# Writing the softmax maxima into the query rows of a strip instead of into a joint buffer

## The reference, cut to what matters

```python
scores = jnp.einsum('bqhd,khd->bhqk', Q, K) * SCALE
attn = jax.nn.softmax(scores, axis=-1)
out = jnp.einsum('bhqk,khd->bqhd', attn, V).reshape(B, QL, HIDDEN)
```

## Time and profile before

| what | value |
|---|---|
| median of 3 runs | 1769.31 us (1768.32 to 1775.3) |
| the profiled execution's own time | 1772.17 us |
| its span | 1770.3 us |
| granted clock of PE, mean | 0.987 |
| PE busy in the span | 96% |
| DVE busy | 79% |
| ACT busy | 65% |
| POOL busy | 30% |

### The profile page before, as it was taken

The page is one execution under the profiler, slowest core; times in us unless marked ns, Lnnn a source line. Parts: engine busy times, 40 slices in busy tenths (PEclk is TensorE's granted clock), DMA queues, the critical chain, the costliest instruction groups (busy, mean ns, idle before and its releaser), DMA issues. The chain is left out here.

```text
span 1770.3 us, 33610 instructions
## 1 busy us (share of the span) xinstructions
PE 1702.0 (96%) x12511; PEld 1045.2 (59%) x12514; DVE 1392.2 (79%) x1930; ACT 1152.1 (65%) x2279; POOL 525.8 (30%) x549
## 2 busy tenths in 40 slices
PE   9999999999999999889999989999999999889998
PEld 6433333333333333655444478888888888768886
DVE  7999999999999995368999667777767777646665
ACT  3788888888888887556888455555545454533333
POOL 7555334344444412011334201211121010142221
PEclk9999999999999999899999999999999999889999
DMA  6322222223322300113546010000000000034332
GB/s 168 55 53 47 57 51 46 46 46 73 69 53 58 71 20 10 37 31 67 134 121 168 29 33 16 24 9 15 23 9 23 15 12 1 19 93 116 104 104 77
DMA packets 50689, 97.48 MB, mean 55 GB/s; under 512 B 11673, under 2 KB 22009, under 8 KB 49131
## 3 DMA queue, kind: packets, MB, share of 16 engines
q1 hardware_dynamic: 50379, 95.58, 22.6%
q10 hardware_dynamic: 192, 0.30, 0.1%
HBM read 64.58 MB, written 15.92 MB: 45 GB/s over the span
## 5 line engine op out<-in xcount | busy, mean ns | idle before, releaser
L1002 ACT ACTIVATE a_probs<-psum 128x512 f32<-128x512 f32 x1280 | 693.3, 597 | 121.9 <-PE psum L770 91.6
L900 DVE TENSOR_REDUCE a_max_part<-psum 128x1 f32<-128x1024 f32 x512 | 621.1, 1223 | 35.9 <-PE psum L706 34.0
L770 PE MATMUL psum<-a_q_max,a_k_rows 51*128 51x512 f32 x1280 | 409.3, 465 | 0.8 <-ACT a_probs L1002 0.7
L749 PE MATMUL psum<-a_probs,a_v_ext 128*32 128x256 f32 (+1 forms) x4600 | 395.1, 415 | 7.0 <-issue 6.9
L706 PE MATMUL psum<-a_k_rows,a_q_rows 48*128 48x512 f32 x1280 | 352.8, 427 | 0.9 <-DVE a_max_part L900 0.9
L770 PEld LDWEIGHTS psum<-a_q_max,a_k_rows 51*128 51x128 f32 x1280 | 167.0, 184 | 270.2 <-ACT a_probs L1002 215.1
L749 PEld LDWEIGHTS psum<-a_probs,a_v_ext 128*32 128x32 f32 x4600 | 91.3, 107 | 206.5 <-issue 105.6
L706 PEld LDWEIGHTS psum<-a_k_rows,a_q_rows 48*128 48x128 f32 x1280 | 151.8, 186 | 13.1 <-issue 3.8
L895 DVE TENSOR_REDUCE a_neg_max<-psum 128x1 f32<-128x1024 f32 x128 | 150.8, 1219 | 8.3 <-PE psum L706 7.9
L2352 PE MATMUL psum<-high_t_parts,high_gu 128*128 128x512 f32 x600 | 150.5, 401 | 6.9 <-POOL high_gu L2470 6.9
L624 POOL TENSOR_TENSOR a_max_bf<-a_neg_max,a_zeros 128x8 bf16<-128x8 f32 x64 | 14.7, 230 | 426.9 <-issue 390.2
(11 more groups left out here) (280 smaller groups left out, 2164.0 us busy)
## 6 DMA issues: line engine op xcount, KB each, us to landing
o<-a_o_out SPq DMA_DIRECT2D x56, 256.0 KB, 2.2
a_k_in<-in_k SPq DMA_DIRECT2D x90, 128.0 KB, 4.6
a_q_rows<-q_high SPq DMA_DIRECT2D x122, 64.0 KB, 2.4
gu_in<-in_w_gu SPq DMA_DIRECT2D x25, 256.0 KB, 2.8
high_cw<-cw SPq DMA_DIRECT2D x22, 256.0 KB, 4.0
a_v_in<-in_v SPq DMA_DIRECT2D x16, 256.0 KB, 5.8
a_o<-o SPq DMA_DIRECT2D x8, 512.0 KB, 4.6
wide_qk_in<-in_wqk SPq DMA_DIRECT2D x16, 256.0 KB, 2.7
```

What stands on the lines that cost most here:

```text
L749: mm = pe.matmul(psum[32 * g:32 * g + 32, 7, cols], self.v_ext[:, b, block_at, :], self.probs[:, j % self.pring, cols], start=(j < 4 and f ...
L770: pe.matmul(psum[:, self.bank_of(self.filling(j)), :], k_rows[rows, b, k0:k0 + P], self.q_max[rows, u % 2, :], start=True, stop=True).then ...
L900: dve.tensor_reduce(self.max_part[:, u % 2, qt, ch:ch + 1], psum[:, 2 * (n % 2):2 * (n % 2) + 2, :], AX.XY, ALU.max).then_inc(self.s1_free, 1)
L1002: act.activation(self.probs[:, p % self.pring, :], psum[:, self.bank_of(self.filling(j)), :], ACT.Exp).then_inc(self.exp_done, 1)
```

## The change

- The three groups of query and key rows move from rows 0 to 47 of a strip to rows 16 to 63 (`FIRST_ROW`). The groups of low and high parts are reordered so that the low key rows still start at 32. Rows 0 to 2 are now those of the maxima.
- `turn_maxima` has no product with the identity; the four bf16 products write 67 rows of the bank. `ident_r` and `q_max` are gone.
- `put_row` copies 3 rows into the first rows of strip 0 of `q_rows` and 3 rows into those of strip 1: two instructions of 512 columns. `row_ready` counts both.
- First and second pass both read all 64 rows of a strip of `q_rows`. In the first pass the rows of the maxima have to be zero, so for each head from the fourth (layer 0) or fifth (layer 1) on, SP issues two more transfers (`zero_maxima`), each of zeros into 3 rows by 1024 columns, right behind the head's six query transfers. PE's wait on `q_loaded` counts them. They are 13 heads in layer 0 and 12 in layer 1.
- At the start of the kernel the selection matrices (`make_pick`) take three DVE copies instead of two, one DVE copy (of `ident_r`) is gone, and the first queries are copied with 128 rows instead of 112 or 115.

```diff
-LOW_K, MROW = 32, 48
-SROWS = MROW + MROWS
-QMAX_ROWS = STRIP + SROWS
+FIRST_ROW, LOW_K = 16, 32
+TURN_ROWS = STRIP + MROWS
...
-            row = STRIP * n + HD * m
+            row = STRIP * n + FIRST_ROW + HD * m
...
+    def zero_maxima(self, sp, b):
+        sp.wait_ge(self.zeros_ready, 1)
+        zero = self.zeros[0:MROWS, 0:P].unsqueeze(1).broadcast_to([MROWS, TT, P])
+        for first in (0, STRIP):
+            sp.dma_start(self.q_rows[first:first + MROWS, b, :].bitcast(F32).rearrange("p (a n) -> p a n", n=P), zero).then_inc(self.q_loaded[b], 16)
...
                     load_q(sp, (0, 1), q_rows[:, got % nb, :], got, self.q_loaded[got % nb])
+                    if got >= nb:
+                        self.zero_maxima(sp, got % nb)
...
-                    pe.wait_ge(self.q_loaded[h % nb], 16 * q_loads * (h // nb + (0 if raw and h % nb == 0 else 1)))
+                    pe.wait_ge(self.q_loaded[h % nb], 16 * (q_loads * (h // nb + (0 if raw and h % nb == 0 else 1)) + 2 * (h // nb)))
...
-                        pe.wait_ge(self.row_ready, u + 2)
+                        pe.wait_ge(self.row_ready, 2 * (u + 2))
...
-                pe.matmul(psum[0:QMAX_ROWS, bank, :], self.ident_r[0:STRIP + MROW, 0:QMAX_ROWS],
-                          q_rows[0:STRIP + MROW, b, half * QH:(half + 1) * QH], start=True, stop=False)
                 pe.wait_ge(self.max_ready, u + 1)
                 for t in range(4):
-                    mm = pe.matmul(psum[0:QMAX_ROWS, bank, t * P:(t + 1) * P], parts[:, 0:QMAX_ROWS], self.ident_bf[:, :], start=False, stop=(t == 3))
+                    mm = pe.matmul(psum[0:TURN_ROWS, bank, t * P:(t + 1) * P], parts[:, 0:TURN_ROWS], self.ident_bf[:, :], start=True, stop=True)
...
-                b, k0, rows = (u // 2) % nb, (j // 2) * P, self.strip_of(j, SROWS)
+                b, half, k0, rows = (u // 2) % nb, u % 2, (j // 2) * P, self.strip_of(j)
                 pe.matmul(psum[:, self.bank_of(self.filling(j)), :], k_rows[rows, b, k0:k0 + P],
-                          self.q_max[rows, u % 2, :], start=True, stop=True).then_inc(self.s2_full, 1)
+                          q_rows[rows, b, half * QH:(half + 1) * QH], start=True, stop=True).then_inc(self.s2_full, 1)
...
-                act.activation(self.q_max[0:QMAX_ROWS, u % 2, :], psum[0:QMAX_ROWS, self.bank_of(self.turn_at), :],
-                               ACT.Copy).then_inc(self.row_ready, 1)
+                b, half = (u // 2) % nb, u % 2
+                for first in (0, STRIP):
+                    act.activation(q_rows[first:first + MROWS, b, half * QH:(half + 1) * QH],
+                                   psum[first:first + MROWS, self.bank_of(self.turn_at), :], ACT.Copy).then_inc(self.row_ready, 1)
...
-                    send_rows(eng, strips, q_rows, (q_high, q_low, q_high), h, None, loaded)
+                    send_rows(eng, strips, q_rows, (q_high, q_high, q_low), h, None, loaded)
```

More of the change, by code:

```diff
@@ L406, in bank_of, with strip_of @@
         return 4 + n % self.ring
-    def strip_of(self, j, rows):
-        return slice(STRIP * (j % 2), STRIP * (j % 2) + rows)
+    def strip_of(self, j):
+        return slice(STRIP * (j % 2), STRIP * (j % 2 + 1))
     def place(self, u, c):
@@ L419, in load_first_k @@
                 part = self.k_dram[0:HD, n * self.per_strip + piece * 512:n * self.per_strip + (piece + 1) * 512]
-                for row in range(STRIP * n, STRIP * n + MROW, HD):
+                for row in range(STRIP * n + FIRST_ROW, STRIP * (n + 1), HD):
                     sp.dma_start(self.k_in[row:row + HD, piece * 512:(piece + 1) * 512], part).then_inc(self.k_first[piece], 16)
@@ L430, in load_k @@
             at = STRIP * n
-            for row in range(0, MROW, HD):
+            for row in range(FIRST_ROW, STRIP, HD):
                 sp.dma_start(self.k_in[at + row:at + row + HD, :], part).then_inc(self.k_loaded, 16)
@@ L507, in make_pick @@
         one = self.ident[0:HD, 0:HD].unsqueeze(1)
[L508 to L511, removed]
+        high = self.pick[:, 0, :].rearrange("p (s r) -> p s r", r=STRIP)
+        low = self.pick[:, 1, :].rearrange("p (s r) -> p s r", r=STRIP)
+        for first in (FIRST_ROW, LOW_K):
+            dve.tensor_copy(high[:, :, first:first + HD], one.broadcast_to([HD, 2, HD])).then_inc(self.pick_ready, 1)
+        dve.tensor_copy(low[:, :, LOW_K + HD:STRIP], one.broadcast_to([HD, 2, HD])).then_inc(self.pick_ready, 1)
     def prepare(self, block):
@@ L704, in first_half @@
                 q0, k0 = half * QH + qt * P, ch * 512
-                rows = self.strip_of(s, MROW)
+                rows = self.strip_of(s)
                 return pe.matmul(psum[:, 2 * (n % 2) + s, :], q_rows[rows, b, q0:q0 + P], k_rows[rows, b, k0:k0 + 512],
@@ L836, in pick_queries @@
                 if half == 0:
-                    pe.wait_ge(self.pick_ready, 2)
+                    pe.wait_ge(self.pick_ready, 3)
                 for m, part in enumerate((projection.highs[0], projection.lows[0])):
-                    mm = pe.matmul(psum[0:STRIP + MROW, bank, :], self.pick[:, m, 0:STRIP + MROW], part[0:HD, 0, cut],
+                    mm = pe.matmul(psum[:, bank, :], self.pick[:, m, :], part[0:HD, 0, cut],
                                    start=(m == 0), stop=(m == 1))
@@ L967, in put_first_queries @@
                 act.wait_ge(self.q_picked, half + 1)
-                act.activation(q_rows[0:STRIP + MROW, 0, half * QH:(half + 1) * QH], psum[0:STRIP + MROW, bank, :],
+                act.activation(q_rows[:, 0, half * QH:(half + 1) * QH], psum[:, bank, :],
                                ACT.Copy).then_inc(self.q_first, 1)
```

25 lines of the change are left out of this document (11 added, 14 removed).

## The result

The changed kernel takes 1782.97 us (median of 6 runs, 1780.74 to 1785.54), the kernel before 1769.35 on the same chip (6 runs, 1768.32 to 1775.3). The ratio is 1.0081, with a 95% interval of 1.0069 to 1.0093: 0.8% slower, 13.6 us. That is beyond the range of the prediction by 1 us, and on the side that had a chance of 0.21.

A forecast was written before the change was run, and what follows sets the result against it. PE was taken to set the pace, until a wait for ACT takes its place. 1772.17 + 2.5 (long stage) + 2.1 (SP's queue) = 1776.8 us profiled; for the median 1769.31 + 4.6 = 1773.9 us, range 1764 to 1782.

The forecast's parts named there:

- What bounds the kernel: Long stage: PE sets the pace; anything taken from PE shortens it until a wait for ACT takes its place.
- Part 2: Second copy on ACT at each turn: 0.49 us more, between nothing and 0.60; hidden in the short stage.
- the turn is shorter: PE's turn, long stage: without the identity product 0.23 us less, at most 0.33.
- chunk 27 behind exponential 25: Long-stage turn: exponential 25 ends at 14.01, chunk 27 would start at 14.04, just met; no loss.
- slot 7 behind the second copy: Long stage: chunk 29 must wait for exponential 26, delayed by the second copy; loss 0.26 us a turn.
- the rest of the half head: Long stage: exponential 28, pushed in the same way, holds chunk 31 by some 0.05 us more.
- The bare load of the first bf16 product: PE's turn: without the identity product, this product pays 0.10 us for a weight load that can't be hidden.
- The two gates behind the second copy: Long stage: exponential 26 holds chunk 29 for 0.26 us, exponential 28 holds chunk 31 for some 0.05.
- the second copy in full: Rival, chunk 29 behind exponential 26: +0.26 us a turn, 8.1 in all, 1779.5 us with the queue; chance 0.19.
- Hidden, with 0.16 to spare: Short stage: the second copy lets ACT start exponential 4 at 908.26, before PE's chunk at 908.42; no cost.
- Part 3: Transfers of zeros in SP's queue: 0.63 us each, 2.1 us once in the short stage, nothing in the long.
- 64 rows at nothing: Products in both passes: 64 rows instead of 48 or 51 cost nothing, as 51 and 112 rows take 0.49.

The follow-up runs named there:

- two_at_zero: The changed kernel with its second copy read from partition 0 and written to a buffer nobody reads, instead of strip 1; ratio 1.0029.
- no_ident: The kernel before without the identity product, so its second pass has no queries, only maxima; one copy, no zeros; ratio 0.9975.
- one_copy: The changed kernel without the copy into strip 1, whose scores then lack their maxima; ratio 1.0006.
- rows64: The kernel before, complete, reading all 64 rows of a strip in both passes instead of 48 and 51; 1772.03 us, one time.

## Why the prediction was wrong

**What bounds the kernel** held: PE sets the pace, and a wait for ACT takes its place.

**Part 2 failed, in its size.** The second copy was taken at 0.49 us, from rows in which every instruction of ACT starts at partition 0. No row had one that starts at 64, and I looked only at the number of rows. The two copies take 1.23 us of ACT instead of 0.98. The table follows a turn of the long stage in the steps of my sum (us; the measured columns are medians over 22 half heads, against the kernel before):

| step | predicted | `two_at_zero` | after |
|---|---|---|---|
| the turn is shorter | -0.23 | -0.30 | -0.30 |
| chunk 27 behind exponential 25 | 0 | +0.10 | +0.10 |
| slot 7 behind the second copy | +0.26 | +0.19 | +0.48 |
| the rest of the half head | +0.05 | +0.02 | +0.03 |
| sum | +0.08 | +0.01 | +0.31 |

The third step is the one that failed: 0.48 us instead of 0.26, of which 0.29 to 0.30 come with the first partition of the second copy. With 31 turns that partition is worth 9.3 us, the whole slowdown of the long stage (+8.7). The chain that I followed (chunk 28 by the copies, chunk 29 by exponential 26) is the one that the trace shows, with one link more: the values behind chunk 29 wait for exponential 27.

At one partition the sum would have been +0.01, 0.07 less than forecast, by three errors that cancel in part, which is luck. The bare load of the first bf16 product costs 0.04 us (the turn of `no_ident`, 0.36, less the 0.32 of the bf16 products before), and 0.02 with the 67 columns of the change, not 0.10. Chunk 27 was "just met" in the forecast and lost 0.10. The two gates behind the second copy were priced at 0.26 and 0.05; the first cost 0.19, the second nothing that shows, as the last 0.02 stand in `one_copy` as well.

**The formula of the Trainium skill** (page "ScalarE: Activation LUTs", section "What ACT_TABLE_LOAD costs") has no term for the number of rows, and the trace agrees: 0.48 us to the next start for 3 and for 115 rows at partition 0, against an estimated 0.52. But its overlap back to back does not hold here for a copy at another first partition than its neighbours': then starts are 0.61 apart, the length of the instruction itself and some.

**The rival nearest to the result** was that of the second copy in full: its place was right, its 0.26 a turn became 0.31, and its 1779.5 us lie 3.5 below the measured time.

**"Hidden, with 0.16 to spare"** fell in the short stage for the same reason: 0.25 more on ACT leave 0.09 uncovered, measured 0.07 a half head, 1.7 us over the stage without zeros.

**Part 3** had the mechanism right, and its size and places off. A transfer of zeros holds the queue for 0.82 us, not 0.63, and PE's loss is 4.1 us, not 2.1. I had it end at half heads 6 to 8, since SP would regain what it lost. It does not in time: copies wait at half heads 6, 8, 10, 20 and 27, and the worst is the one where the late store falls in behind a gather. The first of them, half head 6, waited 1.18 us, not about 2.5. The store that it waits for (the row below) is issued 46.0 us behind the stage's first turn (at 822.5), before 43.0 us (853.06, turn at 810.1), but it landed in 2.2 us (868.44 to 870.64) instead of 3.8.
```profile
868.44 0.41 SPq L151 DMA_DIRECT2D o<-a_o_out  x1
```
The 50 ns for a dispatch in the Trainium skill (page "DMA: Bandwidth & Descriptors", section "Anatomy of one DMA — SWDGE (gpsimd) path") are stated for transfers issued from GpSimd. SP's queue took 0.63 to 0.82 us from issue to issue here, so the figure does not carry over.

**64 rows at nothing** holds within 0.06 us a half head. In the kernel before they cost that much (`rows64`, one profiled execution, 1.8 us in the long stage); in the changed kernel the rest of the half head behind chunk 30 is 0.03 over before, and `no_ident`, without the 64 rows, has the same 0.03.

The sum: 6.2 us too little in the long stage (8.7 - 2.5), 3.7 in the short one (5.8 - 2.1), 9.9 together; the median came out 9.1 above the forecast.

## What to carry to other kernels

A price from a trace holds for the form that the trace shows, and the first partition of source and target belongs to the form: take the distance of starts from rows with the same ones, or give it its own bound. Where one instruction is split into two, ask which engine has idle time at that very place; DVE took the second copy for nothing in the long stage, ACT could not. And a queue that is nearly full does not pay its delay once: follow the store or load behind it to the next gather, and expect its price to differ from kernel to kernel (4.1 to 6.9 us here for the same transfers).

## What the hardware showed that I had not expected

- ACT, copies and exponentials of 512 columns: starts 0.476 to 0.494 us apart when both instructions begin at partition 0, 0.61 on each side of a copy whose source or target begins at 32 or 64 between two that begin at 0; the same for 3 and 51 rows, and for 32 and 64.
- SP's queue, from issue to issue: 0.82 us for 3 rows of zeros from a repeated source of 512 B, 0.735 from plain rows of 4 KB, 0.63 for the 16 rows of a head's loads. Fewer rows and bytes are not cheaper.
- Products with 64 rows instead of 48 and 51 lengthened a slot of the long stage by 0.007 us in `rows64`; in the kernels without the identity product no such difference is seen.
